# A sixteen-batch gather ring in an attention pass, and a later pacing point in the first pass, of a four-layer graph kernel

## What is computed

```
edge_index = stack([src, dst])
x = layernorm(x + L0(x))    # mean of x[src] over each destination, then a matrix
x = layernorm(x + L1(x))    # edge MLP of (x[src], x[dst], weight), maximum over each destination, then an MLP
x = layernorm(x + L2(x))    # a gate per edge from an MLP, then a normalised weighted sum
x = layernorm(x + L3(x))    # attention:
   q, k, v = x@Wq+bq, x@Wk+bk, x@Wv+bv          # 4 heads of 32
   score = einsum(q[dst], k[src]) / sqrt(32)
   p     = exp(score - segment_max(score, dst)[dst])
   alpha = p / segment_sum(p, dst)[dst]
   out   = segment_sum(v[src] * alpha, dst)
   x_r = x@Wskip+bskip;  beta = sigmoid([out, x_r, out-x_r] @ Wbeta);  beta*x_r + (1-beta)*out
```

## Time and profile before

| what | us |
|---|---|
| median of 3 runs | 6286.65 |
| lowest and highest run | 6280.05 and 6288.26 |
| the profiled execution, its own time | 6292.27 |
| its span (first to last instruction) | 6290.4 |
| first pass, about | 0 to 1256 |
| maximum pass, about | 1427 to 2695 |
| gate pass, about | 2871 to 4140 |
| weighted sum, about | 4140 to 4660 |
| attention pass, about | 4765 to 6130 |

### The profile page before, as it was taken

How to read it: one execution, slowest core, us unless ns; L and a number is a source line. 1 busy time by engine, 2 the same in 40 slices (tenths; PEclk the granted TensorE clock), 3 DMA queues, 4 the chain that set the end, 5 groups by cost and what they waited for, 6 DMA issues and landing times. The chain is left out here.

```text
span 6290.4 us, 85261 instructions
## 1 busy us (share of the span) xinstructions
PE 3618.6 (58%) x19084; PEld 2770.9 (44%) x19084; DVE 3432.9 (55%) x6723; ACT 1540.3 (24%) x3649; POOL 3883.9 (62%) x4265
## 2 busy tenths in 40 slices
PE   3444333344555555544777777767744677676763
PEld 2333222232333333333555555556633555555551
DVE  4544222224766666643666666678954455555554
ACT  1110010131222222222222222248841122222224
POOL 6666566656566666656566666668965555555552
PEclk7555555566777777765555555569966666666666
DMA  5555444424555556524555555569954555555551
GB/s 175 167 160 155 140 156 156 156 64 132 170 177 177 175 179 178 178 76 124 144 150 149 150 150 153 150 183 302 313 160 144 158 166 166 163 170 166 165 159 56
DMA packets 810665, 1008.50 MB, mean 160 GB/s; under 512 B 230951, under 2 KB 516017, under 8 KB 810548
## 3 DMA queue, kind: packets, MB, share of 16 engines
q1 hardware_dynamic: 460628, 459.45, 24.8%
q0 software_dynamic: 144320, 323.10, 18.8%
q10 hardware_dynamic: 205600, 224.71, 10.2%
HBM read 645.12 MB, written 361.71 MB: 160 GB/s over the span
## 5 line engine op out<-in xcount | busy, mean ns | idle before, releaser
L518 POOL DMA_INDIRECT L_gath<-tab_kv,src x832 | 789.4, 949 | 572.0 <-issue 243.9
L518 POOL DMA_INDIRECT L_gath<-tab,src x832 | 793.8, 954 | 475.2 <-issue 236.7
L518 POOL DMA_INDIRECT L2a_gath<-tab_h,src x832 | 790.1, 950 | 478.0 <-issue 249.2
L518 POOL DMA_INDIRECT L_gath<-in_x,src x832 | 789.4, 949 | 463.9 <-issue 233.9
L653 ACT ACTIVATE L_back<-L_pB 128x512 f32<-128x512 f32 x624 | 367.8, 590 | 1284.5 <-remote 744.7
L636 DVE TENSOR_TENSOR_SCAN L_acc<-L_mask,L_acc,L_pT 128x512 f32<-128x512 bf16 x207 | 264.4, 1278 | 725.5 <-remote 498.1
L624 PE MATMUL L_pB<-ident,L_acc 128*128 128x128 f32 x2496 | 519.1, 347 | 104.8 <-ACT L_back L653 85.4
L624 PEld LDWEIGHTS L_pB<-ident,L_acc 128*128 128x128 f32 x2496 | 406.2, 184 | 291.1 <-issue 279.9
L1249 PE MATMUL L_pR<-L_pv,L_same 128*128 128x132 f32 x1664 | 378.1, 396 | 267.2 <-DVE L_pv L1327 147.2
L582 PE MATMUL L_pT<-ident,L_gath 128*128 128x128 f32 x832 | 219.5, 417 | 516.1 <-DMA L_gath<-in_x,src 369.3
L853 PE MATMUL L_pM<-L_hid,w_W 128*128 128x512 f32 x416 | 326.3, 878 | 310.9 <-DVE L_acc L890 178.2
(11 more groups left out here) (292 smaller groups left out, 7619.2 us busy)
## 6 DMA issues: line engine op xcount, KB each, us to landing
run<-L_back ACTq DMA_DIRECT2D x416, 256.0 KB
L_seed<-seed SPq DMA_DIRECT2D x416, 256.0 KB
run<-L_back ACTq DMA_DIRECT2D x208, 264.0 KB
seed<-L_zeros SPq DMA_DIRECT2D x208, 256.0 KB
sent<-L2a_gath ACTq DMA_DIRECT2D x208, 256.0 KB
L_sent<-sent SPq DMA_DIRECT2D x208, 256.0 KB
run<-L_back SPq DMA_DIRECT2D x208, 256.0 KB
L_mask<-same SPq DMA_DIRECT2D x208, 128.0 KB
```

The lines of the kernel that those rows point to most:

```text
L518: gp.indirect_dma_start(out=gath[k][:, t, :], out_offset=None, in_=table, in_offset=bass.IndirectOffsetOnAxis(ap=g["src"][:, tile:tile + 1 ...
```

## The change

In the attention pass the ring has sixteen batches (`LONG`), 16 x 4 KB for each partition in place of 8 x 4 KB. GpSimd's first `room` wait is then at batch 16 and asks for `weigh` of the batch sixteen before, not eight before. `same` and all other buffers keep their depth. VectorE's hardware loop, which addresses the ring by its step, has sixteen steps in its body; its stages are the same, in the same order with the same lags. TensorE's, ScalarE's and SyncE's loops keep eight steps. The pacing wait is not touched in this pass. The table `heads` is gone: the query rows pass through the first two `back` buffers, and SyncE writes them out in seven DMAs in place of two. In the first pass `behind` is 15 in place of 11: at a batch's fourth tile GpSimd asks that TensorE has transposed the batch three before, not two.

```
-            gatherer(gp, g, d["x"], gath, s_gath, s_go, s_turn, s_turn, 11)
+            gatherer(gp, g, d["x"], gath, s_gath, s_go, s_turn, s_turn, 15)
...
-    rings = DEEP // SLOTS
+    rings, LONG = DEEP // SLOTS, 2 * DEEP
+    on_deep = lambda f: lambda n, k, r: f(n, k % DEEP, r * (LONG // DEEP) + k // DEEP)
...
-        gath, s_gath, s_go = edge_buffers(ph, 2 * D)
+        gath, s_gath, s_go = edge_buffers(ph, 2 * D, LONG)
...
-        heads = ph.sb("heads", [P, -(-TILES // P), D])
+        head_at = lambda c: back[c // BT][:, c % BT, 0:D]
...
-            sp.dma_start(g["seed"][0:whole * P, :].rearrange("(c p) f -> p c f", p=P), heads[:, 0:whole, :]).then_inc(s_headw, 16)
-            sp.dma_start(g["seed"][whole * P:TILES, :], heads[0:odd, whole, :]).then_inc(s_headw, 16)
-            sp.wait_ge(s_headw, 32)
+            for c in range(whole + 1):
+                count = P if c < whole else odd
+                sp.dma_start(g["seed"][c * P:c * P + count, :], head_at(c)[0:count, :]).then_inc(s_headw, 16)
+            sp.wait_ge(s_headw, 16 * (whole + 1))
...
-                gp.indirect_dma_start(out=heads[0:count, c, :], out_offset=None, in_=g["tab_q"],
+                gp.indirect_dma_start(out=head_at(c)[0:count, :], out_offset=None, in_=g["tab_q"],
...
-                need(v, s_probe, r * rings + k // SLOTS)
+                need(v, s_probe, r * (LONG // SLOTS) + k // SLOTS)
...
-            pipeline(v, BATCHES, DEEP, [(0, pairs), (1, times_key), (1, dot), (2, on_groups(softmax)), (6, weigh), (11, on_groups(gaps)), (12, on_groups(joined))])
+            pipeline(v, BATCHES, LONG, [(0, on_deep(pairs)), (1, times_key), (1, on_deep(dot)), (2, on_deep(on_groups(softmax))), (6, weigh),
+                                        (11, on_deep(on_groups(gaps))), (12, on_deep(on_groups(joined)))])
```

## The result

The changed kernel took 6340.6 us (median of 4, 6329.1 to 6344.9), the kernel before beside it 6287.5 us: a ratio of 1.0084, 95% interval 1.0067 to 1.0102. It is 53 us slower where 53 us faster was forecast. The profiled execution spans 6342.9 us.

What follows compares the result with a forecast made beforehand. GpSimd's gathers and its waits for ring and pace were taken to bound attention; -60 (steady part) + 15 (start) - 8 (first pass) = -53 us, from the median 6286.65 to 6234 us; 8 in 10 between 6170 and 6300.

Steps and rivals of the forecast that it cites:

- What bounds the kernel: Paced part of attention: no engine full; GpSimd first, with 880 us of gathers and 268.8 us of ring and pace waits.
- The steady part: Paced attention, from batch 32: ring waits turn into shorter pace waits, 72 us go; taken as -60 us.
- The start: Attention's unpaced beginning: 64 gathers unbroken in place of 32 while PE and DVE hardly move; +15 us, between 0 and +40.
- The first pass: First pass, later pacing point: longer runs of gathers, less wait for each gather; -8 us, between -20 and +25.
- law of the pause: First pass: GpSimd's pause grows about 0.13 us for each gather in the run, only about 1.2 us fixed.
- The smaller edits: Start of attention: SyncE's five more DMAs, 2.8 us, lie under DVE's preparation; query buffers and longer VectorE loop cost nothing.
- rival D: VectorE's loop of sixteen steps is too long for its instruction store: 6277 us; chance 0.05.
- B: Rival: longer gather runs starve the other engines, at the start and through the whole pass: put at 6310 us; chance 0.13.
- A: Rival: PE and DVE are the bound, pace waits grow by what the ring's shrink: +7, 6294 us; chance 0.16.

Runs made afterwards that it cites:

- before_free_rims: The kernel before (ring of eight), SyncE loading the rims from the table of h without waiting for the group's four stores: ratio 0.9985 to the kernel before.
- ring16_wait8: Changed kernel, but GpSimd still waits for `weigh` of eight batches before and the first pass asks at 11: ratio 1.0000 to the kernel before.
- ring_short_sync: Changed kernel, first pass at 11, SyncE loading masks one batch later and awaiting three of four group stores one batch earlier: ratio 0.9932 to the kernel before.
- before_short_again: Kernel before (ring of eight), masks loaded one batch later, three of four store waits one batch earlier, where the kernel before takes 5212 us: ratio 1.0004.

## Why the prediction was wrong, step by step

**What bounds the kernel: right.** GpSimd's waits, and signals that come late while it issues. The runs without pauses bear it out: same instructions, 1039.5 us in place of 1360.1. One check is off: 880 us of gathers and 269 us of waits make 1149, and less the 0.30 us that each of 100 waits holds anyway 1119, of a stretch of 1140; some 20 us were left unnamed, not 10.

**The steady part: the failing step.** Forecast -60 us, measured +46.0 (1087.0 to 1133.0). The step is "If each ring wait turns into a pace wait, 54 x (3.30 - 1.97) = 72 us go". That GpSimd would go on earlier was right. That the pace wait would then have its old length was not: `spread_dst` is late next, but behind `turn_rims`, which stands ahead of it in PE's queue once in four batches, and whose data comes by way of SyncE. The prediction followed PE's `pD` and not what is queued ahead of it, and took SyncE's work of the pass for free. It leaned on the gate pass, which has no such chain. The pace waits came to 3.42 us in place of 1.97. With SyncE's order changed they are 2.11 us, and the term of -60 is there: 1098.2 to 1038.1 in the steady part, the first being the same order on the ring of eight. Against the 1088.1 of `before_free_rims`, on the same chip, it is -50.

**The start: mechanism right, size near.** +22 us measured for +15, inside 0 to +40. The waits are where they were said to be (idle us ahead of each in brackets):

```profile
4853.69 0.94 POOL L518 DMA_INDIRECT L_gath<-tab_kv,src  x1 [20.17 <-issue]
4874.86 0.94 POOL L518 DMA_INDIRECT L_gath<-tab_kv,src  x1 [6.47 <-DVE L_pv L1329]
```

and 31.7 us at batch 32's second tile, for 20 to 40 forecast. Pacing from batch 8 took the loss away and more.

**The first pass: the size was luck, the step not shown.** The whole came out 9 us shorter with this edit alone, near the 8 forecast, but no profile shows a first pass that is shorter by more than 0.3 us. With the new point and the old one it took 1256.1 and 1250.0 us on the first chip, 1250.8 and 1249.2 to 1251.3 on the second, 1240.9 and 1241.1 to 1243.9 on the third, 1246.3 and 1242.9 on the last. In the changed kernel the runs did get longer, but three waits near 10 us, 64 tiles apart, took that back, where before there was one of 6.1 (the first fence row is the end of a run of twenty, the second the end of one such wait):

```profile
829.70 0.94 POOL L518 DMA_INDIRECT L_gath<-in_x,src  x1 [4.00 <-remote]
865.02 0.94 POOL L518 DMA_INDIRECT L_gath<-in_x,src  x1 [10.67 <-PE L_pT L582]
```

The prediction's law of the pause leaned on single rows. Over the whole first pass before, the median pause is 2.79 us after twelve gathers (22 times), 2.65 after sixteen (15 times, 1.2 to 3.9) and 3.88 after twenty (10 times), so that runs of twenty were there already and 3.30 was one of a wide spread. The long pauses still speak against the fixed 2.0 us that the Trainium skill gives in "DMA: Bandwidth & Descriptors", "Anatomy of one DMA", as the whole of the pause; by the prediction's estimate from it the first pass would have gained 27 us.

**The smaller edits: right.** Nothing, by `ring16_wait8`. SyncE's seven DMAs took 3.58 us, 0.51 each for 0.55:

```profile
4754.87 3.58 SPq L1158 DMA_DIRECT2D seed<-L_back  x7
```

That run also ends rival D, the loop of sixteen.

**The rivals.** B was the truth as far as it went: it says that GpSimd after a stall goes straight on instead of resting until `weigh`, and that PE's stops grow. It named neither SyncE nor the rims. It had 0.13, and its 1.5 us of growth a place rested on no row; PE's wait for the rims alone grew by (161.2 - 39.9)/45 = 2.7 us a group. Its upper price of 6328 was 13 us short of the 6340.6, and the range ended at 6300. A fails, since PE and DVE do go faster in `ring_short_sync`. The chain that was needed stood in the trace of before: `turn_rims` ahead of `pD` in PE's queue, SyncE's load behind five waits, and SyncE's slow steps once GpSimd had gone on.

**What stays open.** The two parts alone multiply to 1.0043, and together they measured 1.0084 and 1.0077. If the 0.9985 of the first pass is left out, since no profile places it, the ring's 1.0058 (to 1.0074) and the whole's intervals (from 1.0067 and 1.0056) overlap, and nothing has to be explained. The single edits ran on another chip than either, and I can't tell the chip's part. Open too is why GpSimd's gathers hold the others back at all.

## What to carry to other kernels

Before a wait is taken away, ask who works while its engine rests: look at each queue that gets ahead in that pause (SyncE's here), and see what would come late if the pause were gone, down to the step that stands ahead of the signal you then wait for. A wait removed and the order it was covering for have to be changed together: neither gained here alone (1.006, 1.003), both gave 0.7%, and with the start paced earlier and the first pass's later point 1.15%. Check a gain at its place too: the first pass's edit made the whole shorter and the first pass not. And run the control on the old kernel, since the same order gave 1.3% on the long ring and cost 0.3% on the short one.

## What the runs showed of the hardware

**The same kernel takes 5212 us at some times and 6214 to 6288 at others.** One and the same chip gave 6217.9 and, some 50 minutes later, 5212.4, medians of 25 and 31 runs. The durations are the same: a gather 0.946 us against 0.949, DVE 3446.9 us busy against 3432.9. PE's granted clock over the execution is 0.68 against 0.64. What differs beside it is that signals are not held back while GpSimd issues its indirect DMAs. At DVE's chain of line 1284, where DVE stood 8.19 and 8.82 us for nothing but itself, the other kind (before_short_again) shows steps without a break:

```profile
4034.08 0.29 DVE L1288 CUSTOM_DVE_ANT_0 L_junk<-xT,L_w_skip 128x128 f32<-128x128 f32 x1
4034.30 0.08 DVE L1288 DVE_READ_ACCUMULATOR2_ANT skip_dot<- 128x1 f32 x1
4034.30 0.28 DVE L1288 CUSTOM_DVE_ANT_0 L_junk<-xT,L_w_skip 128x128 f32<-128x128 f32 x1
```

Its traces also hold 130 thousand records of semaphore updates where the others hold 37 to 39 thousand. What makes the difference can't be told from here, and that the recording of the trace has a part in it is not excluded; that it is not the kernel, nor which chip runs it, can be told.

**SyncE crawls beside a long run of GpSimd's gathers.** Where signals are held, many of SyncE's waits and register instructions take 0.70 to 0.72 us each, and more of them the longer GpSimd has been issuing: in the steady part after, 2% in the first 2 us of a run and 46% from 4 to 10 us on. In GpSimd's pauses 95% take under 0.2 us, with a median of 0.03, and where nothing pauses (before_short_again) none of 1439 takes more than 0.07. The Trainium skill, "Advanced Engine Details and Errata", "Network/Comms", gives 50 to 100 ns for reading a semaphore from a sequencer: the median of 0.03 us in the pauses is no longer than that, the 0.70 us late in a run of gathers is far above it.
